# Rank products moved into the queries' bank, one-time setup spread out, weight loads issued ahead of stores, 39 blocks for 40

## The reference, cut to what matters

```python
x = x + _L0_xattn_ref(_layernorm(x), ctx_2048, ...)    # linear attention, 16 heads, gated
x = x + _L0_ffn_ref(_layernorm(x), ...)                # mixture of 8 experts, top 2, and a shared expert
x = x + _L1_xattn_ref(_layernorm(x), ctx_2048, mask)   # softmax attention, 16 heads
x = x + _L1_ffn_ref(_layernorm(x), ...)                # 256 -> 1024 -> 256, gelu
```

```python
# _L0_xattn_ref, with fm(x) = where(x > 0, x + 1, exp(x))
q, gate = fm(query @ Wq.T), sigmoid(query @ Wg.T + bg)
k, v = split(kv @ Wkv.T);  k = fm(k)
z = 1 / (einsum('bhld,bhd->bhl', q, k.sum(-2)) + EPS)
attn = einsum('bhld,bhde->bhle', q, einsum('bhsd,bhse->bhde', k, v)) * z
out = (attn * gate) @ Wo.T
# _L0_ffn_ref: 256 features, 128 hidden in each expert
scores = xf @ gate_w.T
ew, ei = top_k(scores, 2);  ew = softmax(ew)
expert_out[t, e] = (silu(xf @ w_gate[e].T) * (xf @ w_up[e].T)) @ w_down[e].T
out = sum over the two picked experts of ew * expert_out, plus sigmoid(xf @ se_gate_w.T) * shared(xf)
```

## Time and profile before

| | |
|---|---|
| time, 3 runs | median 404.97 us (404.01 to 405.84) |
| the profiled execution | 404.29 us, its span 402.5 us |
| busy share of the span | PE 93%, PE weight loads 83%, DVE 72%, ACT 61%, POOL 55% |
| mean granted TensorE clock | 0.992 of full speed |
| slots, 0 to 122 us | PE 110.63 us busy, granted clock 0.97 |
| shared expert, 122 to 162 us | PE 38.93 us busy |
| expert blocks, 162 to 232.7 us | PE 66.49 us busy |
| softmax attention, 232.7 to 305 us | PE 67.41 us busy, POOL 59.21 us |
| rest, 305 to 402.5 us | PE 91.81 us busy |

### The profile page before, as it was taken

How to read it: one execution, slowest core, us unless ns; L and a number is a source line. 1 busy time by engine, 2 the same in 40 slices (tenths; PEclk the granted TensorE clock), 3 DMA queues, 4 the chain that set the end, 5 groups by cost and what they waited for, 6 DMA issues and landing times.

```text
span 402.5 us, 10051 instructions
## 1 busy us (share of the span) xinstructions
PE 375.3 (93%) x3270; PEld 333.7 (83%) x3270; DVE 287.9 (72%) x836; ACT 243.8 (61%) x563; POOL 222.8 (55%) x376
## 2 busy tenths in 40 slices
PE   6888999899899999999998999899998989999996
PEld 6667888688687888988898999677766879999996
DVE  4869888778878879754445399877878897684633
ACT  4756776276454352467676687866767778653550
POOL 3556555278767674613341568688887766641100
PEclk9999999799999999999999999999999999999999
DMA  7562212122312145547884441121210000010011
GB/s 242 193 184 65 75 43 74 40 65 75 106 66 92 68 166 191 161 140 237 252 268 148 160 130 55 55 65 58 56 48 17 2 2 2 2 53 28 29 52 54
DMA packets 31460, 38.40 MB, mean 95 GB/s; under 512 B 4401, under 2 KB 28594, under 8 KB 31410
## 3 DMA queue, kind: packets, MB, share of 16 engines
q1 hardware_dynamic: 28338, 29.37, 24.0%
q0 software_dynamic: 3072, 8.39, 6.2%
HBM read 25.03 MB, written 12.71 MB: 94 GB/s over the span
## 4 chain that ended last, share of the span: by engine, by line
PE 52%; DVE 15%; POOL 14%; issue 9%; ACT 4%; DMA 4%; SPq 1%; ACTq 0%; POOLq 0%; DVEq 0%
PE PS L331 8%; PE PS L2224 8%; PE PS L2242 8%; PE PS L333 7%; PE PS L332 7%; POOL rows_early L739 4%; DMA raw<-in_w_l 3%; POOL rj L755 2%; POOL raw L739 2%; PE PS L1962 2%; POOL x L764 2%; PE PS L2282 2%; POOL sj L759 1%; PE PS L2300 1%; PE PS L2059 1%
## 5 line engine op out<-in xcount | busy, mean ns | idle before, releaser
L1078 ACT ACTIVATE arena_f<-PS,cols 128x256 f16<-128x256 f32 x64 | 26.5, 472 | 21.6 <-PE PS L2224 19.1
L331 PE MATMUL PS<-wfh,arena_r 128*128 x120 | 36.0, 300 | 3.3 <-DVE arena_f L1578 1.1
L331 PE MATMUL PS<-w0h,arena_r 128*128 128x256 f32 (+1 forms) x96 | 35.1, 365 | 2.1 <-ACT arena_f L901 1.2
L332 PE MATMUL PS<-wfl,arena_r 128*128 x120 | 33.9, 282 | 0.0
L333 PE MATMUL PS<-wfh,arena_r 128*128 x120 | 33.6, 280 | 0.0
L332 PE MATMUL PS<-w0l,arena_r 128*128 128x256 f32 (+1 forms) x96 | 31.3, 326 | 0.0
L333 PE MATMUL PS<-w0h,arena_r 128*128 128x256 f32 (+1 forms) x96 | 31.3, 326 | 0.0
L2224 PE MATMUL PS<-arena_r,w1h 128*128 128x256 f32 x128 | 31.2, 284 | 0.0
L2224 PE MATMUL PS<-arena_r,w1l 128*128 128x256 f32 x128 | 31.0, 283 | 0.0
L475 POOL TENSOR_TENSOR w1l<-raw,w1h 128x384 fp32r<-128x384 f32 (+1 forms) x14 | 12.7, 912 | 32.5 <-ACT w1h L461 32.5
L696 POOL DMA_INDIRECT xs_rows<-rows_early,posi x24 | 24.7, 1031 | 8.9 <-issue 6.7
(11 more groups left out here) (316 smaller groups left out, 1385.0 us busy)
## 6 DMA issues: line engine op xcount, KB each, us to landing
arena_f<-xs_rows SPq DMA_DIRECT2D x40, 128.0 KB, 2.5
ys_rows<-raw SPq DMA_DIRECT2D x20, 256.0 KB, 2.4
raw<-in_w_ffn SPq DMA_DIRECT2D x16, 241.0 KB, 2.7
raw<-in_w_l SPq DMA_DIRECT2D x12, 192.0 KB, 2.9
ctx_raw<-in_ctxT SPq DMA_DIRECT2D x16, 128.0 KB, 2.0
out<-arena_f SPq DMA_DIRECT2D x7, 256.0 KB, 2.1
raw<-in_w_l SPq DMA_DIRECT2D x5, 256.0 KB, 4.6
x<-in_x SPq DMA_DIRECT2D x1, 1280.0 KB, 6.4
```

The costliest lines, as they stand in the source:

```text
L331: nc.tensor.matmul(out_ap, lh, rh, start=first, stop=False)
L332: nc.tensor.matmul(out_ap, lh, rl, start=False, stop=False)
L1078: nc.scalar.activation(md16[:, g % 2, n, :], PS[:, M_H[n // 2], (n % 2) * D:(n % 2 + 1) * D], ACT.Gelu, bias=cols[:, 2 * KC + n:2 * KC + n ...
```

## The change

It has five parts.

- **Ranks.** `rank_members` of batches 0 and 1 writes to the queries' bank (B_Q) and not to B_TA (RANK_BATCHES = 2). In slots 9 and 13 it stands right behind the gate's bias, ahead of `route`; before, it stood behind the transposes. It waits for ACT's reading of the queries (`q_parts`) and no longer for the router's last scores. The wait for `places` (semaphore `place`) moves from `attended_T` of the same slot to the queries of slots 10 and 14.
- **Setup.** `rwl` stays in slot 3, `below` and `upto8` go to the end of slot 4, and the rest of `setup_late` (eight instructions) goes to the expert blocks, behind pair 0's low part in pass 1 of DVE's loop.
- **SP's order.** In each pass `load_w` stands ahead of `store_block`.
- **39 blocks.** USED = 7 + 32 = 39. The last pair has one block: two block-transposes, six products of `block_in`, one transpose of `block_hT`, three products of `block_down`, one load and half a store are gone. ACT and DVE still read and write the pair at its full width. Counts that others wait for follow (`E["gu"]`: 39).
- ys_rows is one block shorter.

```diff
+USED = EXPERTS - 1 + 2 * TILES
+RANK_BATCHES = 2
+        def ranks(b):
+            at = PS[:, B_Q if b < RANK_BATCHES else B_TA, RANK_AT:RANK_AT + PER_BATCH * EXPERTS]
+            return at.rearrange("p (t e) -> p t e", e=EXPERTS)
...
@@ sync: load_block, store_block and the loop
-                for b, row in enumerate(places.pop(j)):
+                for b, row in enumerate(places.pop(j)[:USED - 2 * j]):
...
-                load(ys_d[2 * j * P:(2 * j + 2) * P, :]...
+                n = min(2, USED - 2 * j)
+                load(ys_d[2 * j * P:(2 * j + n) * P, :]...
...
                 if j + 4 < BPAIRS:
                     load_block(j + 4)
+                if DRAINED + 2 <= j + 1 < SPLITS:
+                    load_w(1, j + 1, (j + 1) % 2)
                 if j >= 2:
                     store_block(j - 2)
-                if DRAINED + 2 <= j + 1 < SPLITS:
-                    load_w(1, j + 1, (j + 1) % 2)
...
@@ vector
+            def route_setup(part):
+                if part == 0:
+                    dve.wait_ge(R["weights_hi"], 1)
+                    nc.vector.tensor_tensor(rwl, ...).then_inc(R["weights"], 1)
+                else:
+                    dve.wait_ge(late_in, 16 * 6)
+                    dve.wait_ge(R["setup"], 4)
+                    nc.vector.tensor_scalar(below[:, :], ...)
+                    nc.vector.tensor_tensor(upto8[:, :, :], ...)
...
-                if s.is_at(3):
-                    setup_late()
+                if s.at in (3, 4):
+                    route_setup(s.at - 3)
...
+                if j == 1:
+                    setup_late()
...
@@ tensor: rank_members
-                pe.wait_ge(R["scores"], scored)
+                if b < RANK_BATCHES:
+                    pe.wait_ge(S0["q_parts"], scored)
+                else:
+                    pe.wait_ge(R["scores"], scored)
...
@@ tensor: slot0, ahead of the queries
                     after(pe, S0["q_parts"], s.pair, 1)
+                    if s.at % PER_BATCH == 2 and s.tile(-2 * PER_BATCH - 2):
+                        pe.wait_ge(R["place"], 4 * (s.at // PER_BATCH - 2) + 1)
...
@@ tensor: slot0, behind the gate
+                if s.at % PER_BATCH == 1 and s.tile(-2 * PER_BATCH - 1):
+                    rank_members(s.at // PER_BATCH - 2, s.at // 2 + 1)
                 if tile := s.tile(-5):
                     route(tile[0])
...
                     route_T(tile[0])
-                if s.at % PER_BATCH == 1 and s.tile(-2 * PER_BATCH - 1):
-                    rank_members(s.at // PER_BATCH - 2, s.at - 4)
                 if tile := s.tile(-2):
                     attended_out(tile[0])
                 if tile := s.tile(-1):
                     if s.at >= 5:
                         pe.wait_ge(R["scores"], s.at - 4)
-                    if s.at % PER_BATCH == 1 and s.tile(-2 * PER_BATCH - 1):
-                        pe.wait_ge(R["place"], 4 * (s.at // PER_BATCH - 2) + 1)
                     attended_T(tile[0])
...
@@ tensor: block_T, block_hT, block_down, block_in
-                for b in range(2):
+                for b in blocks_of(j):      # range(min(2, USED - 2 * j))
```

More of the change, by code:

```diff
@@ L137, in build @@
     xs_d = nc.dram_tensor("xs_rows", (XROWS, D), F32, kind="Internal").ap()
-    ys_d = nc.dram_tensor("ys_rows", (BLOCKS * P, D), F32, kind="Internal").ap()
+    ys_d = nc.dram_tensor("ys_rows", (USED * P, D), F32, kind="Internal").ap()
     with ExitStack() as ctx:
@@ L595, in store_block @@
                 sp.wait_ge(E["y_out"], j + 1)
-                load(ys_d[2 * j * P:(2 * j + 2) * P, :].rearrange("(b p) d -> p b d", p=P),
-                     yb[:, j % 2, :].rearrange("p (b d) -> p b d", b=2), y_stored[j % 2])
+                n = min(2, USED - 2 * j)
+                load(ys_d[2 * j * P:(2 * j + n) * P, :].rearrange("(b p) d -> p b d", p=P),
+                     yb[:, j % 2, 0:n * D].rearrange("p (b d) -> p b d", b=n), y_stored[j % 2])
             sp.wait_ge(tails_zeroed, 16 * (EXPERTS + 1))
@@ L769, in add_delta @@
                 nc.gpsimd.tensor_tensor(x[:, t, :], x[:, t, :], dn[:, t % 3, :], ALU.add).then_inc(x_done[2], 1)
-            pool.wait_ge(E["gu"], 2 * BPAIRS)
+            pool.wait_ge(E["gu"], USED)
             values_setup(4)
@@ L965, in block_silu @@
             def block_silu(j):
-                act.wait_ge(E["gu"], 2 * (j + 1))
+                act.wait_ge(E["gu"], min(2 * (j + 1), USED))
                 if j >= 2:
@@ L991, in ctx_pair_hi @@
                 elif p == 5:
-                    act.wait_ge(E["gu"], 2 * BPAIRS)
+                    act.wait_ge(E["gu"], USED)
                 elif p >= CTX_EARLY:
@@ L1181, in setup @@
                 bias_parts(bg_raw[:, :], 2)
+            def route_setup(part):
+                if part == 0:
+                    dve.wait_ge(R["weights_hi"], 1)
+                    nc.vector.tensor_tensor(rwl, rw_raw[:, :, :], rwh.bitcast(F32),
+                                            ALU.subtract).then_inc(R["weights"], 1)
+                else:
+                    dve.wait_ge(late_in, 16 * 6)
+                    dve.wait_ge(R["setup"], 4)
+                    nc.vector.tensor_scalar(below[:, :], step[:, :], lane[:, 0:1], None, ALU.is_gt)
+                    nc.vector.tensor_tensor(upto8[:, :, :], wide(iota8, 2, EXPERTS), wide(iota8, 1, EXPERTS), ALU.is_ge)
             def setup_late():
-                dve.wait_ge(late_in, 16 * 6)
                 nc.vector.tensor_copy(ident16[:, :], ident[:, :]).then_inc(setup_v, 1)
@@ L1192, in setup_late @@
                 nc.vector.tensor_scalar(lim[:, :], mask_i[:, :], 0.5, 100.0, ALU.is_gt, ALU.mult).then_inc(setup_v, 1)
-                dve.wait_ge(R["weights_hi"], 1)
-                nc.vector.tensor_tensor(rwl, rw_raw[:, :, :], rwh.bitcast(F32),
-                                        ALU.subtract).then_inc(R["weights"], 1)
-                dve.wait_ge(R["setup"], 4)
-                nc.vector.tensor_scalar(below[:, :], step[:, :], lane[:, 0:1], None, ALU.is_gt)
-                nc.vector.tensor_tensor(upto8[:, :, :], wide(iota8, 2, EXPERTS), wide(iota8, 1, EXPERTS), ALU.is_ge)
                 dve.wait_ge(setup_v, 7)
@@ L1283, in places @@
                 done, tiles = R["place"], slice(b * PER_BATCH, (b + 1) * PER_BATCH)
-                rank = PS[:, B_TA, RANK_AT:RANK_AT + PER_BATCH * EXPERTS].rearrange("p (t e) -> p t e", e=EXPERTS)
+                rank = ranks(b)
                 dve.wait_ge(R["rank_psum"], b + 1)
@@ L2050, in _, with blocks_of @@
                         shared_in(2 * g + 3, part)
+            def blocks_of(j):
+                return range(min(2, USED - 2 * j))
             def block_T(j):
-                pe.wait_ge(x_block_in[j % 4], 32 * (j // 4 + 1))
+                pe.wait_ge(x_block_in[j % 4], 32 * (j // 4) + 16 * len(blocks_of(j)))
                 if j >= 2:
                     pe.wait_ge(E["x_lo"], j - 1)
-                for b in range(2):
+                for b in blocks_of(j):
                     for c in range(KC):
```

## The result

The changed kernel takes 394.25 us in the median of 4 runs (393.85 to 395.10), the kernel before 405.40 us (404.01 to 405.87) beside it. The ratio is 0.9725, with a 95% interval of 0.9687 to 0.9764: 11 us faster. The forecast was 394.0 us. The profiled execution took 394.49 us with a span of 392.7 us, 9.8 us less than before.

A forecast was written before the change was run, and what follows sets the result against it. PE was taken to bound the kernel (52% of the chain), held up by others at five places; 0.8 + 3.9 + 1.4 + 3.5 + 1.4 = 11.0 us off the median 404.97 gave 394.0 us, range 391.0 to 399.5.

The forecast's parts named there:

- The slots: Slot 9 to the queries of slot 10: waits, DVE's idle time and half clock go, 3.9 us (2.3 to 4.5).
- What was said of the place: Slot 9: ranks right behind the bias fill PE's 0.46 us wait in front of the router.
- I let all 6.1 through: Way to the blocks: the slots' gains, 0.8 + 3.9 + 1.4 = 6.1 us, all reach the first block.
- slot 13's 1.4: Slot 13: DVE's 1.39 us and PE's 0.79 us of waiting go, taken as 1.4 us (0.8 to 1.6).
- rival 3: Slots 10 to 13: POOL, full of scatters, becomes late; about 3 of 6.1 us left, 397.1 us, chance 0.08.
- The start of the blocks: Before the first block: PE's 0.68 us wait is for the last 16 scatters, which follow the earlier slots.
- Chunk order: Block pairs: chunk loads no longer wait behind the store, so most ACT waits vanish, 3.5 us (0 to 5.0).
- The bound of 5.0: Block pairs: upper bound of the chunk order's gain, all of the ten pairs' excess over 27.9 us.
- Rival 2: Blocks: chunks still come late because landing is the limit; 3.5 less 0.5 us lost, 397.0 us, chance 0.18.
- Setup: Slot 4's queries lose their wait for DVE, 0.8 us (0.4 to 1.24); the setup moved into the blocks costs 0.
- The 1 us more that the prediction left out: Blocks: moved setup on DVE might wait for one POOL memory fill, about 1 us, making the sum 10.0.
- The likeliest case: Whole kernel: forecast as it stands, 391.5 to 396.5 us by its terms' bounds, chance 0.56.

The follow-up runs named there:

- bank_only: Changed kernel with the rank products at their old place behind the transposes, but in the new bank with the new waits: 395.64 us, ratio 0.9754.
- fill13: Changed kernel with POOL's low part of slot 13's weight chunk moved behind the row statistics of slot 14: 393.28 us, ratio 0.9697.
- u_ranks: Changed kernel with the ranks of batches 0 and 1 back in the transposes' bank and behind the transposes: 398.80 us, ratio 0.9837.
- a_order: Kernel before with SP's order alone changed, the chunk's load ahead of the store: 401.76 us, ratio 0.9917.
- pair11: Changed kernel with the last pair's row statistics ahead of the weight chunk's low part on POOL in slot 11: 394.28 us, ratio 0.9740.
- a_ranks: Kernel before with the ranks' part of the change alone: 401.22 us, ratio 0.9898.

## Why the prediction was right

**The slots.** Right in mechanism. In slot 9 the wait, DVE's idle time and the clock's fall all went: 4.2 us against 3.9. What was said of the place was wrong: the ranks filled the router's wait, but the kernel with the old place and the new bank is as fast in the slots. The gain is the bank's, with its waits.

**The step that failed** is "I let all 6.1 through", with slot 13's 1.4. Between slots 10 and 13 0.85 us was given back, because POOL's statistics stand behind a chunk's low part (rival 3 in small, at another price: 0.85 and not 3), and slot 13 gave 0.68, because places that no longer wait for PE fell onto POOL's low part. The trace of before had the stall in reach. The slow cast of `posy` was put down to it in the part on the setup, and the member table's cast in slot 12 had it as well (0.17 us in slot 8):

```profile
101.00 1.33 DVE L1261 CAST top_f<-top_i 128x8 f32<-128x8 uint32 x1
```

But it was not asked what DVE's places would meet at their new time. At the first block 4.94 us were left of 6.1.

**The start of the blocks** was misread. The 0.68 us ahead of the first block were put to the scatters. They are PE's first load of offsets, as the runs with fewer values show. The time came out none the worse: the block followed the slots all the same, 51.18 us behind the queries of slot 14 (51.16 before).

**Chunk order.** 2.9 us in the trace (3.5 undone, 1.3 alone beside 40 blocks) for a forecast of 3.5. The bound of 5.0 was mis-sized: 2.1 us of excess are left in the changed trace, all in passes with loads of offsets, which no order on SP removes. So about 3, or little more, were to be had by the order, and they came nearly whole. Rival 2 did not happen here, but stands next in line, as the runs with fewer values per load show: thinned loads alone gave nothing in these pairs.

**39 blocks** gave 1.6 us for 1.4 (1.9 undone). **Setup** gave 1.0 to 1.35 in slot 4 for 0.8, and cost 0.2 in the blocks, which were taken as free; net it is near the forecast. The 1 us more that the prediction left out did not come: the eight instructions ran in 0.15 to 0.23 us each, from 166.87 on, when POOL's last fill was ending (166.90).

**The whole.** The terms give 9.8 us where 11.0 were forecast, while the medians differ by 11.15. The profiled execution of before was one of its faster ones: 404.29 us at a mean clock of 0.992, where eleven others, beside the runs from bank_only to fill13, had 0.978 to 0.992 and a median of 405.54 us. So in most executions of before the lower clock cost more than in the one that was read; in which stretches, no trace shows. The time came out within 0.3 us of the forecast with an overestimate in the terms (11.0 for 9.8) and an underestimate in the base. That the two cancel is luck.

The likeliest case, 391.5 to 396.5 us, is said to follow from the bounds of the terms. These add up to 4.5 and 13.9 us, from 400.5 to 391.0 us: its slow end was narrower than the working allows.

Of the signs named ahead, the queries of slot 4, the ranks behind the bias (0.11 us), the clock in slots 9 and 10 and ACT's waits (2.2 us) came as said, and the queries of slot 10 came 5.13 us earlier for 4.5 to 5. The first block (157.06 for 156), the pairs (30.00 for 29.5) and the first gather (223.47 for 221.8) are late by about what the failed steps lack.

## What to carry to other kernels

When a wait goes, look at what the freed engine meets at its new time: here the places ran into an instruction of POOL that held them up for its whole length, and the member table of slot 13, ready 0.17 us ahead of its use (98.56 and 98.73), was late once something else was mended. Before an excess is put to one cause, subtract what repeats with a period of its own (here every fourth pass). To learn whether a move or a resource made a gain, undo one of the two: in the slots the bank with its waits was worth 4 us, the place nothing.

## What was not expected of the hardware

PE's clock fell to the lower level in stretches of two lengths, about 3.4 us and 6.8 us. With the ranks in the old bank it fell behind their wait in all three profiles taken (before, u_ranks, a_order: 6.8, 3.5 and 6.8 us), and with the new bank in none of the others at that place, but in several it fell elsewhere: near 8 us in the start (in eight traces), at 99.5 us (pair11, behind PE's wait of 0.72 us), at 254 (a_ranks, 6.8 us) and at 296 us (bank_only).

Loading 16 values to PE's registers cost a pass 0.4 to 0.9 us, 8 values 0 to 0.7, and 4 values nothing in most passes (lengths of the passes less 2.79 us).

DVE's small instructions took up to eleven times as long beside POOL: the cast 1.34 us and 1.95 against 0.17, the second step of the places 1.36 against 0.23, and in each of these the DVE instruction ended within 0.1 us of POOL's.
